# Quantised feed-forward kept in integers, up ahead of gate, GpSimd out of it; first queries' root from the norm's variance; tables loaded early

## What is computed

```
def act_qdq(x):
    scale = jnp.maximum(jnp.max(jnp.abs(x)) / qmax, 1e-12)
    return jnp.clip(jnp.round(x / scale), -qmax - 1.0, qmax) * scale
x = act_qdq(x)
up = act_qdq(x @ lpbq_dequant(w_up).T)
gate = act_qdq(x @ lpbq_dequant(w_gate).T)
sig = fixed_qdq_u16(jax.nn.sigmoid(gate))
gate = act_qdq(gate * sig)
o = act_qdq(gate * up)
return o @ lpbq_dequant(w_down).T
...
x = x + _L0_ffn_ref(_layernorm(x), ...)
x = x + _L1_xattn_ref(_layernorm(x), ctx_1024, ...)
...
sn = rmsnorm(slots, slot_norm_w)
q_proj = sn @ Wq.T
```

## Time and profile before

| what | us |
|---|---|
| three timed runs | 883.88, 875.12, 880.88 |
| their median | 880.88 |
| the profiled execution, its own time | 883.04 |
| its span, from first to last instruction | 880.8 |
| outside the span | 2.24 |

### The profile page before, as it was taken

One profiled execution on the slowest core, in us unless ns is written; L12 is line 12 of the kernel. 1 busy time (PEld: TensorE's weight loads), 2 busy tenths in 40 slices (PEclk: granted clock), 3 DMA queues, 4 the chain that ended last, 5 costly groups with the idle time before them and its releaser, 6 DMA issues.

```text
span 880.8 us, 24033 instructions
## 1 busy us (share of the span) xinstructions
PE 739.6 (84%) x8992; PEld 496.6 (56%) x8992; DVE 582.9 (66%) x1064; ACT 547.0 (62%) x1166; POOL 425.9 (48%) x496
## 2 busy tenths in 40 slices
PE   5778999999999999998570557888788876799997
PEld 2254666666666666665230337877788765344443
DVE  4975777777777777761458556767866774656563
ACT  3354666666666666664036349888987893355554
POOL 1859566666666666600004003444554431266664
PEclk9798999999999999999775877989988998799999
DMA  6315344444444444230210320542444241121200
GB/s 194 90 54 176 89 125 124 122 122 122 122 122 122 122 122 122 52 77 2 103 68 0 123 95 2 197 169 73 147 146 147 75 162 57 36 72 36 72 1 22
DMA packets 26288, 85.60 MB, mean 97 GB/s; under 512 B 5524, under 2 KB 7060, under 8 KB 26212
## 3 DMA queue, kind: packets, MB, share of 16 engines
q1 hardware_dynamic: 26216, 84.63, 30.2%
HBM read 65.72 MB, written 0.46 MB: 75 GB/s over the span
## 4 chain that ended last, share of the span: by engine, by line
PE 53%; DVE 15%; POOL 11%; issue 9%; ACT 8%; DMA 2%; SPq 1%; POOLq 0%; DVEq 0%; ACTq 0%
PE ps L1214 8%; POOL ctx_lo L579 8%; PE ps L1244 7%; PE ps L1231 7%; PE ps L1432 5%; ACT c_prob L723 4%; PE ps L1201 4%; PE ps L1190 4%; PE ps L1418 3%; DVE tile_max L809 2%; PE ps L1324 2%; PE ps L1248 2%; ACT w0T L723 2%; PE ps L1178 2%; PE ps L1169 1%
## 5 line engine op out<-in xcount | busy, mean ns | idle before, releaser
L809 DVE TENSOR_REDUCE tile_max<-ps 128x1 f32<-128x500 f32 x336 | 214.8, 675 | 74.7 <-PE ps L1214 73.9
L602 ACT ACTIVATE probs<-ps 125x896 f32<-125x896 f32 x192 | 176.1, 917 | 106.4 <-PE ps L1231 106.1
L1214 PE MATMUL ps<-k_hi,qdiag 128*128 128x500 f16 x336 | 130.9, 392 | 12.3 <-DVE tile_max L809 11.0
L723 ACT ACTIVATE c_prob<-ps,c_bias,row_scale 125x56 f32<-125x56 f32 x384 | 116.0, 490 | 0.7 <-DVE c_bias L1042 0.4
L1231 PE MATMUL ps<-qstack,kstack 98*125 98x224 f16 x768 | 108.4, 263 | 0.4 <-issue 0.2
L579 POOL TENSOR_TENSOR ctx_lo<-ctx_hi,ctx_lo 128x448 f16<-128x448 f32 x64 | 72.2, 1128 | 70.7 <-ACT ctx_lo L768 70.7
L1231 PEld LDWEIGHTS ps<-qstack,kstack 98*125 98x125 f16 x768 | 86.8, 138 | 19.9 <-issue 5.6
L1244 PE MATMUL ps<-probs,v_aug 125*25 125x168 f32 x1536 | 94.2, 317 | 0.5 <-ACT probs L602 0.5
L556 POOL TENSOR_TENSOR c_prob<-c_prob,c_weight 125x672 f32<-125x672 f32 x32 | 42.0, 1312 | 104.5 <-DVE c_weight L1056 104.5
L484 POOL TENSOR_TENSOR qstack<-q_rep,slot_mask 96x224 f16<-96x224 f32 (+1 forms) x64 | 34.2, 563 | 85.5 <-PE ps L1231 83.2
L1486 PE MATMUL ps<-ctx_lo 128*128 128x448 f16 x192 | 68.5, 357 | 6.7 <-DVE ctx_hi L1152 3.0
(11 more groups left out here) (224 smaller groups left out, 1755.9 us busy)
## 6 DMA issues: line engine op xcount, KB each, us to landing
row_tiles<-in_ctx_rows_wide SPq DMA_DIRECT2D x40, 774.0 KB, 5.7
ctx<-in_ctxT SPq DMA_DIRECT2D x16, 750.0 KB, 5.4
rows_in<-in_ctx_rows SPq DMA_DIRECT2D x16, 750.0 KB
kstack<-k_hi SPq DMA_DIRECT2D x128, 93.8 KB, 2.7
kstack<-k_lo SPq DMA_DIRECT2D x64, 93.8 KB, 2.7
ctx_hi<-in_wg SPq DMA_DIRECT2D x8, 256.0 KB, 2.6
ctx_hi<-in_wu SPq DMA_DIRECT2D x8, 256.0 KB, 3.0
ctx_hi<-in_wd SPq DMA_DIRECT2D x8, 256.0 KB, 3.7
```

What stands on the lines that cost most here:

```text
L602: nc.scalar.activation(probs[c % 3][0:CH, :].rearrange("p (k w) -> p k w", k=2), score_tile(c)[0:CH], ACT.Exp, scale=float(HD) ** -0.5 / W ...
L723: last = nc.scalar.activation(c_prob[n % PROBS][:, c, :], ps[0:CH, 2 * (n % 2) + c // 6, bass.ts(c % 6, TOK)], ACT.Exp, bias=c_bias[n % 2] ...
L809: nc.vector.reduce_max(tile_max[:, u % MAXT, u // MAXT:u // MAXT + 1], ps[:, MAXB + (u + p) % 2, 0:KCOLS], AX.X).then_inc(max_done, 1)
L1214: nc.tensor.matmul(ps[:, MAXB + (u + p) % 2, 0:KCOLS], qdiag[p][:, bass.ts(t, 128)], k_hi[p][:, bass.ts(j, KCOLS)], start=True, stop=True) ...
```

## The change

1. Integers stay integers. Gate, up and the products are rounded but not scaled back; the factors are carried in small tiles: `q_unit` (a scale's reciprocal in units of the tile that it is applied to) and `q_step_up` (the product of the steps). The sigmoid takes gate's scale as its own factor, and the last scale is applied where the down product is added to `xT`.
2. Up's six products come before gate's six. VectorE takes up's maxima and scale first, then gate's, and rounds two tiles of gate; ScalarE rounds the third, takes the three sigmoids (the third tile first), and then rounds up.
3. GpSimd does nothing in the feed-forward. VectorE does all three tiles, with a maximum behind each.
4. The reciprocal of the root that the first queries need comes from norm 2's variance v directly. In the reference the slots are (x-m)/sqrt(v+e) and their mean square is v/(v+e), so that the two norms together are (x-m)/sqrt(v(1+r)+er), with e = 1e-5 and r = 1e-6. One root with scale 1 + r and bias er gives it; `centred_b` is multiplied by it, and `stream` itself is made later (`first_stream` behind unit 1 on VectorE, `late_spread` behind unit 1's scores on TensorE).
5. `keep_busy` products stand in three more places: five ahead of the first scale's spreading, two behind the merged weights, eight behind norm 2's variances. They write bank 5 in place of 6.
6. The sigmoid's table is loaded behind norm 1's root, the exponential's behind norm 2's roots and ahead of `query_hi`.
7. The half biases `half_b` are made behind the rounding of `stream`.

```
-            load_table(ACT.Sigmoid)
-            for f in range(F0):
-                nc.scalar.activation(sig[:, f, :], gate[:, f, :], ACT.Sigmoid).then_inc(sig_done, 1)
+            act.wait_ge(scale_done, 3)
+            magic_added(gate[:, last, :], q_inv[:, 2:3])
+            magic_removed(gate[:, last, :], last_gate_rounded)
+            act.wait_ge(last_gate_rounded, 1)
+            nc.scalar.activation(sig[:, last, :], gate[:, last, :], ACT.Sigmoid, scale=q_scale[:, 2:3]).then_inc(sig_done, 1)
...
+            magic_added(up, q_inv[:, 1:2])
+            magic_removed(up, up_rounded)
...
+            nc.scalar.activation(first_sd_rows, ps[:, 2, 0:GW], ACT.Sqrt, bias=eps_both[:], scale=1.0 + RMS_EPS).then_inc(first_sd, 1)
+            act.wait_ge(ln_rstd, 2)
+            nc.scalar.activation(sd[:], ps[:, 2, 0:GW], ACT.Sqrt, bias=eps_ln[:]).then_inc(ln_sd, 1)
+            load_table(ACT.Exp)
...
+            for i, f in enumerate((last, *range(last))):
+                dve.wait_ge(sig_done, i + 1)
...
                 chain(nc.vector.tensor_scalar(sig[:, f, :], sig[:, f, :], MAGIC_16, MAGIC_16 + TOP_16, ALU.add, ALU.min))
                 chain(nc.vector.scalar_tensor_tensor(out=gate[:, f, :], in0=sig[:, f, :], scalar=MAGIC_16, in1=gate[:, f, :], op0=ALU.subtract, op1=ALU.mult))
+                part_max(3, i, gate[:, f, :])
+            scale_of(3, F0)
+            in_units_of(3, q_scale[:, 2:3])
+            chain(nc.vector.tensor_scalar(gate[:, 0:last, :], gate[:, 0:last, :], q_unit[:, 3:4], MAGIC, ALU.mult, ALU.add))
             dve.wait_ge(up_rounded, 1)
+            chain(nc.vector.scalar_tensor_tensor(out=gate[:, 0:last, :], in0=gate[:, 0:last, :], scalar=MAGIC, in1=up[:, 0:last, :], op0=ALU.subtract, op1=ALU.mult))
+            part_max(4, 0, gate[:, 0:last, :].rearrange("p f t -> p (f t)"))
+            dve.wait_ge(gated_rounded, 1)
+            chain(nc.vector.scalar_tensor_tensor(out=gate[:, last, :], in0=gate[:, last, :], scalar=MAGIC, in1=up[:, last, :], op0=ALU.subtract, op1=ALU.mult))
+            chain(nc.vector.tensor_scalar(q_step_up[:, 0:1], q_scale[:, 3:4], q_scale[:, 1:2], None, ALU.mult))
+            chain(nc.vector.tensor_scalar(q_step_up[:, 4:5], q_step_up[:, 0:1], 1.0 / QMAX, None, ALU.mult))
+            part_max(4, 1, gate[:, last, :])
             scale_of(4, 2)
+            in_units_of(4, q_step_up[:, 0:1])
+            rounded(gate[:, 0:last, :], q_unit[:, 4:5], dve_out, 1)
...
+                if n == 1 and k == SLOTS - 1:
+                    first_stream()
```

More of the change, by code:

```diff
@@ new lines, in _ @@
+            act.wait_ge(unit_done, 1)
+            nc.scalar.activation(gate[:, last, :], gate[:, last, :], ACT.Identity, bias=magic[:, 0:1], scale=q_unit[:, 3:4]).then_inc(gated_rounded, 1)
+            act.wait_ge(unit_done, 2)
+            magic_added(gate[:, last, :], q_unit[:, 4:5])
+            magic_removed(gate[:, last, :], out_rounded)
+            load_table(ACT.Sqrt)
+            _, centred, squared, _ = NORMS[2]
+            for h in range(2):
+                act.wait_ge(ln_centred, 4 + h + 1)
+                nc.scalar.activation(squared[:, bass.ts(h, HALF)], centred[:, bass.ts(h, HALF)], ACT.Square).then_inc(ln_squared, 1)
@@ L976, in _ @@
             nc.vector.tensor_scalar(half_b[:], half_b[:], 0.5, None, ALU.mult).then_inc(merged, 1)
-            part_max(0, 0, stream[:])
-            scale_of(0, 1)
-            rounded(0, stream[:], stream_rounded, 1)
-            copied_maxima(1, gate)
-            for f in range(F0):
-                rounded(1, gate[:, f, :], gate_rounded, f + 1)
-            copied_maxima(2, up)
-            for f in range(F0 - 1):
-                dve.wait_ge(sig_done, f + 1)
+            copied_maxima(1, up)
@@ L987, in _ @@
+            copied_maxima(2, gate)
+            last = F0 - 1
+            for f in range(last):
+                rounded(gate[:, f, :], q_inv[:, 2:3], gate_rounded, f + 1)
+            chain(nc.vector.tensor_scalar(q_step_up[:, 3:4], q_scale[:, 2:3], 1.0 / QMAX, None, ALU.mult))
+            for i, f in enumerate((last, *range(last))):
+                dve.wait_ge(sig_done, i + 1)
+                if f == last:
+                    dve.wait_ge(last_gate_rounded, 1)
                 chain(nc.vector.tensor_scalar(sig[:, f, :], sig[:, f, :], MAGIC_16, MAGIC_16 + TOP_16, ALU.add, ALU.min))
@@ L1021, in _ @@
[L1021 to L1026 removed]
+            for h in range(2):
+                at = bass.ts(h, HALF)
+                dve.wait_ge(ln_mean, 4 + h + 1)
+                nc.vector.tensor_tensor(centred_b[:, at], xT[:, at], ps[:, h, 0:HALF], ALU.subtract).then_inc(ln_centred, 1)
@@ new lines, in _ @@
+            dve.wait_ge(first_sd, 1)
+            nc.vector.reciprocal(first_root, first_sd_rows).then_inc(first_inv, 1)
+            dve.wait_ge(ln_sd, 3)
+            nc.vector.reciprocal(rstd[:], sd[:]).then_inc(ln_rstd, 1)
+            dve.wait_ge(ln_centred, 6)
+            for h in range(2):
+                at = bass.ts(h, HALF)
+                dve.wait_ge(first_spread, h + 1)
+                nc.vector.tensor_tensor(squared_b[:, at], centred_b[:, at], ps[:, FIRST_SPREAD + h, 0:HALF], ALU.mult).then_inc(first_slots, 1)
@@ L1031, in _, with first_stream @@
             dve.wait_ge(rms_inv_done, 2)
+            def first_stream():
+                for h in range(2):
+                    at = bass.ts(h, HALF)
+                    dve.wait_ge(ln_spread, 4 + h + 1)
+                    nc.vector.tensor_tensor(stream[:, at], centred_b[:, at], ps[:, LATE_SPREAD + h, 0:HALF], ALU.mult).then_inc(ln_out, 1)
+                dve.wait_ge(ln_out, 6)
+                nc.vector.memset(ps[:, UPD, 0:2 * (D + 1)], 0.0).then_inc(merged, 1)
             def logits_shift(n):
```

143 lines of the change are left out of this document (68 added, 75 removed).

## The result

The changed kernel takes 868.12 us (median of 4 runs, 864.86 to 869.84), the kernel before on the same chip 879.42 (4 runs, 875.12 to 883.88). The ratio is 0.9858, with a 95% interval of 0.9819 to 0.9897: faster by 1.4%, where 870 us were forecast. The profiled execution took 869.84 us.

A forecast was written before the change was run, and what follows sets the result against it. VectorE nearly sets the feed-forward's pace; 500 to 518 us is pure latency. Terms -4.0 + 0.05 - 9.0 + 0.7 = -12.2 gave 870.8 from the profiled 883.04, 868.7 from the median; forecast 870 us, range 864.5 to 877 (8 in 10).

The forecast's parts named there:

- Step 1: Ahead of gate and up's products: moving the half biases off the path saves 0.27 us.
- Step 2: First six feed-forward products: unread products keep 2.4 GHz, copies come 0.75 us apart; a lost clock costs up to 2.6 us.
- Step 3: Gate's maxima and scale: VectorE goes straight through six maxima (3.9 us) and the scale (2.1), ready at 462.1.
- Step 4: Rounding, sigmoids, gating: VectorE and ScalarE meet near 465.2, then three tiles at 0.72 + 1.12 + 1.12 us, 8.9 in all.
- Step 5: Scales 3 and 4 up to the down product: it starts at 489.1 for 493.07; steps 1 to 5 give -4.0 us.
- Step 6: Norm 2's first reciprocal to the first unit: 6.3 us for 14.9; with faster first scores -9.0, about -6.8 without the clock.
- Step 7: Exponential's table load moved ahead of `query_hi`: gives nothing and costs nothing.
- Step 8: `stream` made later, among the first units: ScalarE waits about +0.7 us once, bounds 0 and 1.6.
- the clock is not kept: Rival for feed-forward and norm 2: too few unread products, 2.6 and 2.2 us lost, -7.4 us and 875.6; chance 0.20.
- More than forecast: Rival: full clock through the first units as well, -15 us, 868; chance 0.15.
- slower: Rival: the clock falls in each group of units from 520 to 740 us, 895 at a mean of 0.78; chance 0.03.
- the last rival: ScalarE's third-tile rounding meets the sigmoids late by a whole pass, gain 11 us; counted inside the forecast case, no own chance.

The follow-up runs named there:

- experiments 2 to 4 and 7: experiment 2, experiment 3, experiment 4, and the changed kernel with gate's products, maxima and scale ahead of up's again, 864.36 us in one run.
- experiment 4: The changed kernel with four GpSimd multiplications on a dead tile added beside VectorE's gating, from the first sigmoid on; 871.90 us in one run.
- the second profile: Profile of the unaltered changed kernel timed again, on the chip of the kernels with filled norms; 867.93 us (6 runs), ratio 0.9856 to the kernel before.
- experiment 2: The changed kernel without the eight unread products behind norm 2's variances; 868.01 us in one run.
- experiment 3: The changed kernel with the sigmoid's and the exponential's table loads put back where they were; 865.77 us in one run.
- experiment 5: The kernel before with norm 2's part alone (root from variance, eight unread products, early exponential table, late stream); 870.33 us (10 runs), ratio 0.9897.
- experiment 1: The changed kernel without the five unread products ahead of the first scale and the two behind the merged weights; 870.46 us in one run.
- experiment 11: The changed kernel with gate ahead of up and unread products in norms 1 and 3 and ahead of scales three to five; 856.33 us, ratio 0.9714.

## Why the prediction held, step by step

- **Step 1** (half biases, -0.27): -0.24. The first filling ended at 444.25, before the diagonal's product at 444.50, as taken. From output projection to P six executions of this order (the changed kernel twice, experiments 2 to 4 and 7) took 18.15 to 18.60 us, so that a hit to 0.03 is luck.
- **Step 2** (full clock): held; copies are 0.75 us apart. Lost, it costs 2.85, and 2.6 was the bound.
- **Step 3** (gate's scale 14.1 us after the products begin): VectorE's first use of it is at 460.92, 13.7 after P.
- **Step 4** (three tiles of 2.96): 2.91. The 0.68 was read from the first L987 as if it ran alone, but GpSimd's L536 ran beside it; the same operation took 0.63 in the changed kernel (L1006). The pass that only subtracts also takes 0.63, within the bounds of 0.6 and 0.75. That GpSimd's absence counts is shown by experiment 4: put back for 8.25 us, GpSimd costs 2.41. But VectorE also took over GpSimd's tile, and by the table below the two cancel. The expectation of experiment 4 had the place wrong: not L987 in particular is slowed, but whatever operation of that kind VectorE begins during one of GpSimd's with two inputs.
- **Step 5** (down product 41.1 after P): 41.13, 41.50 in the second profile. From the end of the last maximum of the three tiles (473.05) to the down product it took 15.3 us where 14.9 were counted, and that used up the 0.4 us of step 3. The two small errors cancel in the 41.13.
- **Step 6** (6.3 from reciprocal to first unit, -9.0 in all): 504.05 - 498.02 = 6.03, and -9.13. The mis-sized term is the clock's: 2.2 if lost, 1.14 measured. The 2.2 has no working in the prediction. A query product at 1.49 and the first scores would be 0.77 + 0.3 of it, and these never came due: in experiment 2 the clock was back at 0.99 for the query products, and only the spreading was slow.
- **Step 7** (tables, nothing): nothing, by experiment 3.
- **Step 8** (+0.7 as a wait of ScalarE): the wait is 0.28. VectorE's three pieces took 1.24, 1.45 and 1.00 where 4.2 us were counted in all. The whole stretch is 0.80 longer, but it differed by 3.5 us between seven executions of the same units (223.08 to 226.60), so that this near hit is luck.

The rivals: "the clock is not kept" fell by the copies and windows, and would have cost 2.85 + 1.14 = 4.0 of the 12.3, not 4.8. "More than forecast" and "slower" both needed another clock in the units, which stayed at 0.89. ScalarE did come late to the sigmoids, by 0.52 us, less than the whole pass of the last rival. What I did not see is how far the means of the rival reach: norms 1 and 3 stood in the same profile with spreadings of 3.35 us, twice what they take at 2.4 GHz, and filling these gaps gave another 0.9756 / 0.9856, 1.0%.

What each edit gave inside the feed-forward can be read from the rows. Hours of VectorE after P, and of the down product; the third column is the old feed-forward in experiment 5, the fourth the new one without its unread products:

| event, us after P | before | experiment 5 | experiment 1 | changed |
|---|---|---|---|---|
| first scale ready | 10.49 | 9.41 | 10.96 | 7.97 |
| gating begins | 20.86 | 19.78 | 20.14 | 17.14 |
| third scale ready | 31.59 | 30.52 | 30.97 | 27.98 |
| down product | 44.81 | 43.74 | 43.98 | 41.13 |

Of the 3.68 us, 2.52 come before the first scale, and that is the clock. From there to the gating it is 1.20 less (10.37 against 9.17), which is 0.9 for the third tile's rounding moved to ScalarE (the wait of 0.52 counted in) and 0.29 in the second scale. The gating itself, up to the third scale, is 0.11 longer: without GpSimd no operation is held up, but VectorE does a third tile (0.63 + 1.09 with their gaps), and that costs about what the wait of L987 (2.53 less 0.63) gave back. The rest is 0.07 less. So the new order by itself is worth 0.8 to 1.3 us (34.3 us from first scale to down product in both old executions, 33.0 in experiment 1, 33.2 and 33.5 in the two of the changed kernel), and with its clock lost the new stage took as long as the old one in experiment 5. What integers, tiles and GpSimd give one by one was not tried in runs of their own.

## What to carry to other kernels

Where engines hand a small piece to and fro, look at the granted clock of that window beside TensorE's durations: products of twice their length there are cured by a few unread products in the wait ahead of them, sized to end before the real work is ready, since those that outlast it delay it by as much (experiment 11). Where two norms follow each other, look for the second's root in the first's variance: taking it out was most of norm 2's part, which gave about two thirds of this gain. Where VectorE sets the pace, an operation with two inputs on GpSimd can hold it up by its whole length; weigh that against the work that VectorE takes over, which here came out even. Judge a stretch of small pieces by more than one execution, since the clock moved unchanged stretches by 1.1 and 1.5 us; and don't spend effort on moving table loads that lie in ScalarE's idle time.

## What the runs showed of the hardware

That VectorE waits for a whole GpSimd operation I had only as one row of 2.53 us; experiment 4 gives it twice more, with 2.23 for 1.09. The wait goes the other way too: L541 below began while VectorE's L999, with two inputs, ran to 484.30, and took 2.91, where the same kind of multiplication took 2.07 in L538. Not every GpSimd operation holds VectorE up. In the kernel before, L987 and L988 took 0.68 and 1.09 us (469.12 and 469.83) where the changed kernel has 0.63 and 1.09. They ran during L536, which has a single tensor input; the profile of experiment 5 shows the same durations there. Timeline of GpSimd, whose records are rough:

```profile
468.39 2.46 POOL L536 TENSOR_SCALAR work<-work 128x896 f32<-128x896 f32 x1
...
483.32 2.91 POOL L541 TENSOR_TENSOR row_tiles<-row_tiles 128x896 f32<-128x896 f32 x1 [10.31 <-ACT row_tiles L696]
```
